# Second layer of a four-layer graph stack on one core: sum beside turn, and W_h beside W_t, as single products of 256 columns, two graphs to a bank

## What is computed

```python
in_degrees = jnp.sum(jnp.abs(adj), axis=-1)
norm = ((in_degrees + 1e-06) ** (-0.5))[..., None]
f_hom = jnp.einsum('bnd,de->bne', x, theta) * norm
f_hom = jnp.einsum('bnm,bmd->bnd', adj, f_hom) * norm
f_het = jnp.einsum('bnd,de->bne', x, W_h)
gate = jax.nn.sigmoid(jnp.einsum('bnd,de->bne', x, W_t) + b_t)
out = gate * f_hom + (1.0 - gate) * f_het
return jax.nn.elu(out)
```

## Time and profile before

| | before |
|---|---|
| median of three runs | 735.71 us |
| profiled execution: time / span | 734.84 us / 733.0 us |
| PE busy / instructions | 684.8 us (93%) / 4226 |
| weight loads (PEld) busy | 587.3 us (80%) |
| DVE, ACT, POOL busy | 564.6, 541.5, 300.4 us |
| mean granted TensorE clock | 0.994 |
| chain that ended last | PE 55%, DVE 19%, ACT 14% |

### The profile page before, as it was taken

One profiled execution on the slowest core, in us unless ns is written; L12 is line 12 of the kernel. 1 busy time (PEld: TensorE's weight loads), 2 busy tenths in 40 slices (PEclk: granted clock), 3 DMA queues, 4 the chain that ended last, 5 costly groups with the idle time before them and its releaser, 6 DMA issues.

```text
span 733.0 us, 12659 instructions
## 1 busy us (share of the span) xinstructions
PE 684.8 (93%) x4226; PEld 587.3 (80%) x4226; DVE 564.6 (77%) x1362; ACT 541.5 (74%) x1167; POOL 300.4 (41%) x427
## 2 busy tenths in 40 slices
PE   3999899989999989989999999989999998989986
PEld 2787788879888779878978868879878887978766
DVE  4689986888978886789988886798886786787334
ACT  5577788668788878667878978657888768647653
POOL 4322435464335443573244534573334225642412
PEclk9999999999999999999999999999999999999999
DMA  6520011200000020410000020110000000110001
GB/s 162 126 80 1 2 30 32 58 1 4 6 4 1 1 61 2 130 44 2 5 7 1 2 61 1 59 59 2 6 6 1 1 1 1 58 58 5 9 1 58
DMA packets 47624, 21.10 MB, mean 29 GB/s; under 512 B 9032, under 2 KB 47560, under 8 KB 47560
## 3 DMA queue, kind: packets, MB, share of 16 engines
q1 hardware_dynamic: 47560, 20.29, 10.3%
HBM read 15.27 MB, written 4.19 MB: 27 GB/s over the span
## 4 chain that ended last, share of the span: by engine, by line
PE 55%; DVE 19%; ACT 14%; issue 6%; POOL 4%; DMA 1%; DVEq 0%; SPq 0%; POOLq 0%; ACTq 0%
PE bank L404 9%; PE bank L406 9%; PE bank L405 9%; PE bank L399 6%; DVE rh L1353 3%; PE bank L390 3%; ACT x_in L704 2%; ACT xn L704 2%; DVE bank L1356 2%; PE bank L592 2%; PE bank L604 2%; PE bank L607 2%; POOL rstd L945 2%; ACT rh L901 2%; PE bank L555 2%
## 5 line engine op out<-in xcount | busy, mean ns | idle before, releaser
L961 POOL TENSOR_TENSOR h_lo<-h,h_hi 128x512 fp32r<-128x512 f32 x64 | 82.6, 1291 | 243.2 <-ACT h_hi L876 243.2
L1353 DVE SCALAR_TENSOR_TENSOR rh<-bank,rh 128x512 f32<-128x512 f32 x80 | 55.0, 688 | 87.0 <-ACT bank L909 86.9
L404 PE MATMUL bank<-h_hi,whh_hi 128*128 128x512 f32 x240 | 105.8, 441 | 12.9 <-DVE rh L1353 11.9
L404 PE MATMUL bank<-g_hi,wc_hi 128*128 128x512 f32 x240 | 102.6, 427 | 0.0
L406 PE MATMUL bank<-h_lo,whh_hi 128*128 128x512 f32 x240 | 95.0, 396 | 0.0
L405 PE MATMUL bank<-h_hi,whh_lo 128*128 128x512 f32 x240 | 94.5, 394 | 0.0
L406 PE MATMUL bank<-g_lo,wc_hi 128*128 128x512 f32 x240 | 94.4, 393 | 0.0
L405 PE MATMUL bank<-g_hi,wc_lo 128*128 128x512 f32 x240 | 93.7, 391 | 0.0
L399 PEld LDWEIGHTS bank<-edge,hn 128*128 128x128 f32 x640 | 83.6, 191 | 8.4 <-DVE edge L1061 2.0
L915 ACT ACTIVATE bank<-bank,bih 128x512 f32<-128x512 f32 x80 | 52.9, 661 | 45.2 <-DVE bank L1356 45.1
L399 PE MATMUL bank<-edge,hn 128*128 128x128 f32 x640 | 84.3, 274 | 1.6 <-DVE edge L1061 1.6
(11 more groups left out here) (168 smaller groups left out, 1668.1 us busy)
## 6 DMA issues: line engine op xcount, KB each, us to landing
x_in<-in_x SPq DMA_DIRECT2D x8, 512.0 KB, 5.4
adj_in<-in_adj SPq DMA_DIRECT2D x8, 512.0 KB, 5.0
x_res<-in_x SPq DMA_DIRECT2D x16, 256.0 KB, 2.8
out_x<-x_res SPq DMA_DIRECT2D x16, 256.0 KB, 2.3
xz<-x_res SPq DMA_DIRECT2D x16, 50.0 KB
w_sb<-in_L_gnn_W SPq DMA_DIRECT2D x1, 640.0 KB, 5.2
w_sb<-in_L_gnn_W SPq DMA_DIRECT2D x5, 128.0 KB, 5.1
rows<-in_adj SPq DMA_DIRECT2D x32, 0.6 KB
```

What stands on the lines that cost most here:

```text
L404: nc.tensor.matmul(dst[:], w_hi, m_hi, start=start, stop=False)
L961: nc.gpsimd.tensor_tensor(h_lo[q][:], h[q][:], h_hi[q][:].bitcast(f32), ALU.subtract).then_inc(sem["h_lo_new"], 1)
L1353: nc.vector.scalar_tensor_tensor(rh[:], R_BANK[:], 1.0, rh[:], ALU.add, ALU.mult).then_inc(sem["rh_ready"], 1)
```

## The change

Identity is kept as a seventeenth matrix behind `adjT`, and one product of each graph streams `[adjT of the graph | identity]`, 256 columns, through the weights `xn`: the sum and the turned graph come out side by side. Two graphs fill a bank: graphs 0 and 1 of the quad go to `A_BANK`, 2 and 3 to `B_BANK`. ACT copies each bank to half of a tile `sh` (128 x 4 x 256, two of them). In the second part one product of each graph streams `[W_h | W_t]`, 256 columns, through the turned half; the first pair goes to `A_BANK`, the second to `C_BANK`, each with its own bias product over the W_t columns, and ACT reads each bank with a tanh and a copy of 256 columns. The product with theta stays as it was.

```diff
-        adjT = sb("adjT", [128, RG, 128])
+        adjT = sb("adjT", [128, RG + 1, 128])
...
+        sh = [sb(f"sh{i}", [128, QUAD, 256]) for i in range(2)]
...
                 keep_busy(r, (14, 0, 8, 5)[q])
+                pe.wait_ge(sem["identity_beside"], 1)
                 pe.wait_ge(sem["ln1_xn"], u + 1)
+                pe.wait_ge(sem["adjT_scaled"], u + 1)
                 if q:
                     pe.wait_ge(sem["l1_het"], u)
                 elif r:
                     pe.wait_ge(sem["ln3_h"], u)
-                for j in range(QUAD):
-                    last = nc.tensor.transpose(A_BANK[:, j * 128:(j + 1) * 128], xn[:, q * QUAD + j, :], ident[:])
+                for j in range(2):
+                    b = q * QUAD + j
+                    last = nc.tensor.matmul(A_BANK[:, j * 256:(j + 1) * 256], xn[:, b, :], adjT[:, b:RG + 1:RG - b, :],
+                                            start=True, stop=True)
                 last.then_inc(sem["ln1_turned"], 1)
-                pe.wait_ge(sem["adjT_scaled"], u + 1)
                 if q:
                     pe.wait_ge(sem["l1_diff"], u)
                 elif r:
                     pe.wait_ge(sem["l3_scaled"], u)
-                for j in range(QUAD):
-                    last = nc.tensor.matmul(B_BANK[:, j * 128:(j + 1) * 128], xn[:, q * QUAD + j, :],
-                                            adjT[:, q * QUAD + j, :], start=True, stop=True)
+                for j in range(2):
+                    b = q * QUAD + 2 + j
+                    last = nc.tensor.matmul(B_BANK[:, j * 256:(j + 1) * 256], xn[:, b, :], adjT[:, b:RG + 1:RG - b, :],
+                                            start=True, stop=True)
                 last.then_inc(sem["l1_s"], 1)
...
-                else:
-                    pe.wait_ge(sem["l1_gate"], u)
-                nc.tensor.matmul(C_BANK[:], ones_r[:], bias_row(0), start=True, stop=False)
-                pe.wait_ge(sem["ln1_h"], u + 1)
+                for pair, dst, read, made in ((0, A_BANK, "ln1_h", "l1_gate_lin"), (2, C_BANK, "l1_s_read", "l1_het_lin")):
+                    pe.wait_ge(sem[read], u + 1)
+                    if q and pair:
+                        pe.wait_ge(sem["l1_het"], u)
+                    for j in range(2):
+                        nc.tensor.matmul(dst[:, j * 256:(j + 1) * 256], sh[q % 2][:, pair + j, 128:256], wl1[:, 128:384],
+                                         start=j == 0, stop=False)
+                    nc.tensor.matmul(dst[:].rearrange("p (b d) -> p b d", b=2)[:, :, 128:256], ones_r[:],
+                                     bias_rows[:, 0, :].unsqueeze(1).to_broadcast([128, 2, 128]), start=False, stop=True
+                                     ).then_inc(sem[made], 1)
-                for j in range(QUAD):
-                    last = nc.tensor.matmul(C_BANK[:, j * 128:(j + 1) * 128], hT[q % 2][:, j, :], wl1[:, 256:384],
-                                            start=False, stop=j == QUAD - 1)
-                last.then_inc(sem["l1_gate_lin"], 1)
-                for j in range(QUAD):
-                    last = nc.tensor.matmul(A_BANK[:, j * 128:(j + 1) * 128], hT[q % 2][:, j, :], wl1[:, 128:256],
-                                            start=True, stop=True)
-                last.then_inc(sem["l1_het_lin"], 1)
-                pe.wait_ge(sem["l1_s_read"], u + 1)
                 for j in range(QUAD):
-                    last = nc.tensor.matmul(B_BANK[:, j * 128:(j + 1) * 128], sT[:, j * 128:(j + 1) * 128], wl1[:, 0:128],
+                    last = nc.tensor.matmul(B_BANK[:, j * 128:(j + 1) * 128], sh[q % 2][:, j, 0:128], wl1[:, 0:128],
                                             start=True, stop=True)
...
             def l1_read_turned(r, q):
                 u = r * QUADS + q
+                if u >= 2:
+                    act.wait_ge(sem["l1_hom"], u - 1)
                 act.wait_ge(sem["ln1_turned"], u + 1)
-                nc.scalar.activation(hT[q % 2][:], quad(A_BANK[:, :]), ACT.Copy).then_inc(sem["ln1_h"], 1)
+                nc.scalar.activation(sh[q % 2][:, 0:2, :], A_BANK[:].rearrange("p (b d) -> p b d", b=2), ACT.Copy
+                                     ).then_inc(sem["ln1_h"], 1)
                 act.wait_ge(sem["l1_s"], u + 1)
-                if u:
-                    act.wait_ge(sem["l1_hom"], u)
-                nc.scalar.activation(sT[:], B_BANK[:], ACT.Copy).then_inc(sem["l1_s_read"], 1)
+                nc.scalar.activation(sh[q % 2][:, 2:4, :], B_BANK[:].rearrange("p (b d) -> p b d", b=2), ACT.Copy
+                                     ).then_inc(sem["l1_s_read"], 1)
...
-                nc.scalar.activation(gate_th[:], C_BANK[:], ACT.Tanh, scale=0.5).then_inc(sem["l1_gate"], 1)
-                act.wait_ge(sem["l1_het_lin"], u + 1)
-                nc.scalar.activation(hetS[:], A_BANK[:], ACT.Copy).then_inc(sem["l1_het"], 1)
+                for src, c in ((A_BANK, slice(0, 2)), (C_BANK, slice(2, 4))):
+                    if src is C_BANK:
+                        act.wait_ge(sem["l1_het_lin"], u + 1)
+                    pair = src[:].rearrange("p (b d) -> p b d", b=2)
+                    gate = nc.scalar.activation(quad(gate_th[:])[:, c, :], pair[:, :, 128:256], ACT.Tanh, scale=0.5)
+                    het = nc.scalar.activation(quad(hetS[:])[:, c, :], pair[:, :, 0:128], ACT.Copy)
+                gate.then_inc(sem["l1_gate"], 1)
+                het.then_inc(sem["l1_het"], 1)
...
+            def identity_beside():
+                nc.vector.tensor_copy(adjT[:, RG, :], ident[:]).then_inc(sem["identity_beside"], 1)
...
                 if slot == 7:
+                    identity_beside()
                     shares()
```

## The result

The changed kernel takes 739.85 us (median of 10 runs, 738.62 to 741.36) where the kernel before takes 735.49 in the same comparison (10 runs): the ratio is 1.0063, interval 1.0053 to 1.0073, or +4.4 us. The forecast was +4.5 on 735.71. The profiled execution took 739.99 us, its span 738.2.

A forecast was written before the change was run, and what follows sets the result against it. PE was taken to bound 12 of 16 quads beside the GRU, an ACT and DVE loop the tail. +4.0 beside the GRU and +0.5 in the tail, on a median of 735.71, gave 740.2 us, range 736.8 to 743.0.

The forecast's parts named there:

- The bound: Second layer beside the GRU: in 12 of 16 quads a microsecond of PE work is a microsecond of the end.
- Price of a pass: PE products: a pass of 256 columns costs 0.22 us, twice one of 128; the gap between streamed blocks costs nothing.
- W_h with W_t: PE's linear products per quad: joined they cost 1.76 us instead of 1.78, -0.02.
- split bias: PE's bias in two products of 256 columns instead of one of 512: taken as nothing extra, at most +0.24 us.
- Turn with sum: PE's turn and sum joined, per quad: 1.76 us instead of 1.32, +0.44, as the turn takes two passes.
- The rival at 720 us: PE: weight loads were the price, 256-column passes go at 0.11 us, 1.3 us less a quad; chance 0.05.
- Beside the GRU: 12 quads at +0.42 us of PE, 5.0, less 1.0 of waits ahead of the sum in three rounds: +4.0 us.
- The stalls stay: Behind each stretch PE's two stalls, 0.64 and 0.57 us, stay, because DVE's mix needs ACT's exponential, tied to PE.
- The rival that the stalls swallow the change: Behind each stretch DVE's chain does not move, 1.2 us a round comes back, +0.9 left: 736.6 us; chance 0.13.
- Tail: ACT and DVE loop of 5.9 us binds; three loops 0.12 us longer each and a later first gate: +0.5 us.
- the first gate: In the tail, the first gate waits some 0.15 us longer for `diff`, which needs theta.
- Sum: Whole kernel: 4.0 beside the GRU plus 0.5 in the tail, +4.5 us, giving 740.2 us.

The follow-up runs named there:

- pairs_front_only: Kernel before with only two graphs to a bank, turned half by transposes; linear products and ACT reads essentially as before; ratio 1.0018.
- turn_as_product: Kernel before with one edit: each graph's turn is a product with identity instead of a transpose, nothing joined; ratio 1.0084.
- joined_split_again: Changed kernel with every product of 256 columns put as two of 128, same banks and reads; ratio to the kernel before 1.0077.
- after_exp_ahead: Changed kernel with ACT's relu and exponential of a round's first three quads moved ahead of norms and `H_BANK` read, beside the GRU; ratio to before 1.0014.
- before_exp_ahead: Kernel before with ACT's relu and exponential of a round's first three quads moved ahead of norms and `H_BANK` read, beside the GRU; ratio 0.9959.
- reads_in_halves: Kernel before with only ACT's tanh and copy of the second layer cut into two instructions of 256 columns each; ratio 1.0011.
- pairs_front_exp_all: Kernel before with two graphs to a bank, turned half by transposes, and ACT's exponential moved ahead beside the GRU and in the tail; ratio 0.9999.

## Why the prediction was right, point by point

**Result.** 740.2 was forecast, 739.85 measured; +4.5 against +4.4 us, on the slower side by more than the noise.

**The bound.** Right that PE is on the end in 12 of 16 quads, but only half the picture: the chain through DVE, POOL and ACT ends with it, for 0.32 us of waits taken off PE moved the end by 0.04 at most (`pairs_front_only`). More PE work comes out at the end, as `turn_as_product` shows with 1.4 us a stretch for 4 x 0.47 = 1.9 of work, less the covered waits; covered waits alone do not.

**Price of a pass.** 0.22 forecast, 0.216 measured; the two blocks with a gap cost nothing (0.86 to 0.87 us for four passes, as for W_h with W_t, which lie side by side), and neither does the split bias (0.12 each). Turn with sum: +0.44 forecast, 2 x 0.87 - 1.32 = +0.42 measured. W_h with W_t: -0.02 forecast, and with the bias 1.96 against 2.02, -0.06 measured. Sum +0.36 instead of +0.42.

**Weight loads.** The page "TensorE: Matmul & The Clock Gate" of the Trainium skill, section "LDWEIGHTS (loading the stationary operand)", gives 107 ns for a load of 128 columns. In `joined_split_again` 16 loads more cost 0.12 us a quad, 0.0075 each, so nearly all of a load is hidden here. The rival at 720 us would have needed 1.3 us a quad, some ten times that. The section "Terms" of the same page of the Trainium skill, with transpose mode four times faster for FP32, is not borne out: 0.43 us against 0.90 in `turn_as_product`, twice.

**Beside the GRU.** Forecast 4 x 0.42 - 0.32 = 1.36 us a round, measured 0.96 in the two undisturbed rounds. The term that is too large is mostly PE's work: 4 x 0.36 = 1.44, less 0.32 is 1.12; the stalls behind the stretch gave back another 0.06. The 0.1 left is not placed. By this sum the covered waits did count, and for a reason that I had not given: in the changed kernel PE sets the chain up to 365, so what it saves is saved. In the kernel before the same waits are worth nothing (`pairs_front_only`).

**The stalls stay.** Right, and in the changed kernel by the link given, which the chain of waits shows and `after_exp_ahead` cuts. For the kernel before, from whose rows the link was read, it did not hold: the `mix` at 364.12 starts when DVE's own `mv` is done, while `ex` (363.29, 0.63 us long) ended at 363.92. The 1.05 us of "issue" ahead of rh in the earlier trace rows are DVE at work on a slow `mix`, and the `gated` of 1.78 is a second slow one; the prediction took them as they stood. The rival that the stalls swallow the change did not come.

**Tail.** Forecast +0.5, measured +0.86. The loops are right, +0.12 and +0.13. The mis-sized term is the first gate, put at +0.15: from the read of `H_BANK` in step 79 to it the time grew by 0.50 (671.31 - 666.44, less the 4.37 us by which that step began later). The first quad's second layer, on PE and with a wait for the copy of the first bank (its L499 takes 1.08 us on the chain where the next takes 0.86), came on the chain there.

**Sum.** The traces give 3 x 0.96 + 0.86 = 3.7 us, the times 4.4, interval 3.9 to 5.4. So the closeness of 740.2 is in part luck: some 1.1 too much beside the GRU, 0.4 too little in the tail, and some 0.7 that the undisturbed stretches do not show. The steps between them do not give it either (0.25 shorter in all); the start of the changed kernel's trace is 1.05 longer, and no run shows whether that belongs to the change.

## What to carry to other kernels

Before two products are joined, price each by passes and columns: a transpose that runs as one pass becomes two when it is made by a product with identity, and the streaming of a wider product is hardly cheaper than of two narrow ones (0.216 us against 2 x 0.112 here). Where one engine is without gaps, ask whether another chain ends just beside it: here added work came out at once, and saved waits did not until the second chain was cut as well. The cut was to move one pair of ACT instructions from behind a read that it did not need, and it was worth more (4.0 us) than the join with transposes (0.5 us, not clear of the noise). When an instruction on such a chain takes over twice its usual time, look at what another engine does at that moment: an edit can help by changing which of the two starts first.

## What the runs showed that was not expected

DVE and POOL hold each other up, and this makes the second chain long. In the kernel before DVE waits for ACT's exponential 0.41 us at 345.03 and 0.17 at 354.85, and not at 364.04 (the `mix` of 364.12 in the earlier trace rows). But twice a DVE instruction that otherwise takes 0.69 us takes about 1.8: `mix` (L1215) at 356.91 and `gated` (L1212) at 365.34. Both start just behind the start of POOL's `h_lo`. In `before_exp_ahead` DVE starts first, its instruction takes 0.69 us, and POOL's is the long one (1.79 instead of about 1.28). DVE and POOL in order of time, the kernel before and then `before_exp_ahead`:

```profile
365.20 1.36 POOL L961 TENSOR_TENSOR h_lo<-h,h_hi 128x512 fp32r<-128x512 f32 x1 [5.40 <-ACT h_hi L876]
365.34 1.77 DVE L1212 SCALAR_TENSOR_TENSOR gated<-gate_th,diff 128x512 f32<-128x512 f32 x1
```

```profile
365.57 0.69 DVE L1219 SCALAR_TENSOR_TENSOR mix<-gated,hetS 128x512 f32<-128x512 f32 x1
365.61 1.79 POOL L965 TENSOR_TENSOR h_lo<-h,h_hi 128x512 fp32r<-128x512 f32 x1 [6.00 <-ACT h_hi L877]
```

This holds throughout: of the 416 `gated` and `mix` (the `mix` that is made from `gated`) in the 13 traces, the 96 that start within 0.9 us behind the start of an `h_lo` take 1.01 to 1.81 us, and the other 320 take 0.67 to 0.77. So moving the exponential in the kernel before took away waits and also two times 1.1 us of DVE in the last two steps of a stretch; no run parts the two. In the changed kernel they are parted: with and without the move one such instruction is left near the end (`mix` with 1.80, `gated` with 1.77), and the move still gains 0.7 to 0.8 us a stretch.

The granted clock of PE falls to its lower level, 1.2 of 2.4 GHz, in twelve of the 13 profiled executions (not in that of `joined_split_again`) ahead of the last microseconds, in which all 13 have it, and in one to three of the same four places: near 20 us in ten, near 87 us in five, near 322 us in two and near 491 us in two. In the changed kernel's profile (busy time by stretch, PEclk is the granted share):

```profile
320.00:323.00 3.00, 1.62 (x6) 1.08 (x7) 2.18 (x7) 2.52 (x5) 2.86 (x4) 1.00 0.32 93
323.00:326.00 3.00, 3.00 (x13) 2.47 (x12) 2.97 (x9) 2.57 (x5) 3.00 (x2) 0.52 0.01 3
```

Just before it PE was busy only 1.62 of 3 us, with an idle time of 1.35 us:

```profile
322.32 0.50 PE L404 MATMUL bank<-h_hi,whh_hi 128*128 128x512 f32 x1 [1.35 <-DVE rh L1367]
```

The turn of the next state behind it takes nearly twice its usual time (1.06 for the row of four instead of 0.60), and this stretch is 1.67 us longer instead of 0.96: the fall cost 0.7 us. `turn_as_product` has one at the same place of the next round (a share of 0.53 from 493 to 496 us, behind an idle time of 1.36), with the same 0.7 us; the kernel before has the same idle time there (1.35 us at 489.53) and no fall. A fall does not always cost that much: in `reads_in_halves` the stretch with one is only 0.3 us longer than its other two, and in `pairs_front_exp_all` it is 0.3 us shorter; in both, two slow DVE instructions (about 1.45 and 1.65 us) that the other two stretches have are gone. A fall of 0.7 us is 0.1% of the time and makes part of the scatter in which a change of this size is measured, but not all: of the changed kernel's ten runs the slowest, 741.36 us, had a mean granted clock of 0.995 and the fastest, 738.62 us, 0.994.
